# One transformer layer on one core: the LoRA rows transposed a tile later, next to the token transposes

## What is computed

```python
xA = jnp.einsum('bld,edr->bler', x, A)
xAB = jnp.einsum('bler,erd->bled', xA, Bm) * scale
return (xAB * w).sum(axis=2)
...
gate = x @ W_gate + _lora(x, sA_gate, sB_gate, scale) + _expert_lora(x, A_gate, B_gate, w, scale)
```

## Time and profile before

| what | value |
|---|---|
| median of 3 runs | 669.27 us (669.23 to 669.83) |
| profiled execution, its own time | 669.42 us |
| its span, first to last instruction | 667.6 us |
| TensorE busy | 659.3 us, 99% of the span |
| VectorE busy | 376.3 us, 56% |
| ScalarE busy | 257.8 us, 39% |
| GpSimd busy | 127.1 us, 19% |
| stage 1 on TensorE | about 8.9 to 128.9 us, tiles of 7.1 us (odd) and 8.0 us (even) |

### The profile page before, as it was taken

How to read it: one execution, slowest core, us unless ns; L and a number is a source line. 1 busy time by engine, 2 the same in 40 slices (tenths; PEclk the granted TensorE clock), 3 DMA queues, 4 the chain that set the end, 5 groups by cost and what they waited for, 6 DMA issues and landing times.

```text
span 667.6 us, 10326 instructions
## 1 busy us (share of the span) xinstructions
PE 659.3 (99%) x3568; PEld 545.4 (82%) x3568; DVE 376.3 (56%) x698; ACT 257.8 (39%) x413; POOL 127.1 (19%) x290
## 2 busy tenths in 40 slices
PE   7999999999999999999999999999999999999998
PEld 6899998877767788888888888888888888888886
DVE  6677888778676955434355443445344326534433
ACT  5434444566326323332343333243233324333321
POOL 3565676627336320000000000000000000000000
PEclk9999999999999999999999999999999999999999
DMA  6876665743745669930025000021400001300001
GB/s 215 311 256 212 214 235 194 261 183 149 292 170 196 236 183 3 77 128 0 1 79 221 32 0 0 0 75 72 184 0 0 0 8 71 127 0 0 0 0 63
DMA packets 41643, 74.21 MB, mean 111 GB/s; under 512 B 19393, under 2 KB 20289, under 8 KB 39953
## 3 DMA queue, kind: packets, MB, share of 16 engines
q1 hardware_dynamic: 38672, 64.52, 34.2%
q10 hardware_dynamic: 2736, 9.05, 3.4%
q0 software_dynamic: 208, 0.30, 0.3%
HBM read 52.81 MB, written 21.04 MB: 111 GB/s over the span
## 4 chain that ended last, share of the span: by engine, by line
PE 94%; DVE 3%; DMA 1%; ACT 1%; issue 0%; POOL 0%; DVEq 0%; POOLq 0%
PE bank L1246 21%; PE bank L1248 21%; PE bank L1247 21%; PE bank L1491 18%; PE bank L1464 6%; DVE den L1092 2%; PE bank L1477 1%; PE bank L1475 1%; PE bank L1265 1%; PE bank L1277 1%; DMA w_raw<-in_wkT 1%; PE bank L1364 1%; PE bank L1502 1%; PE bank L1504 1%; PE bank L1286 0%
## 5 line engine op out<-in xcount | busy, mean ns | idle before, releaser
L1246 PE MATMUL bank<-x,up_h 128*128 128x512 f32 (+1 forms) x352 | 137.1, 389 | 0.2 <-DVE x3r L1057 0.2
L1247 PE MATMUL bank<-x,up_h 128*128 128x512 f32 (+1 forms) x352 | 137.0, 389 | 0.0
L1248 PE MATMUL bank<-x,up_l 128*128 128x512 f32 (+1 forms) x352 | 137.0, 389 | 0.0
L1183 DVE TENSOR_TENSOR hf<-bank,silu 128x512 f32<-128x512 f32 x44 | 30.4, 691 | 155.0 <-issue 135.3
L1491 PE MATMUL bank<-dn,hid_h 128*128 128x512 f32 x352 | 108.8, 390 | 0.0
L677 ACT ACTIVATE hid_h<-hf 128x512 fp32r<-128x512 f32 x44 | 27.8, 632 | 144.1 <-DVE hf L1183 144.1
L1246 PEld LDWEIGHTS bank<-x,up_h 128*128 128x128 f32 x352 | 66.1, 188 | 14.4 <-issue 0.7
L1491 PEld LDWEIGHTS bank<-dn,hid_h 128*128 128x128 f32 x352 | 65.8, 188 | 14.5 <-DVE res L1208 0.6
L1248 PEld LDWEIGHTS bank<-x,up_l 128*128 128x128 f32 x352 | 66.1, 188 | 13.8
L1247 PEld LDWEIGHTS bank<-x,up_h 128*128 128x128 f32 x352 | 66.1, 188 | 13.7
L888 DVE TENSOR_TENSOR up_l<-up_raw,up_h 128x1024 fp32r<-128x1024 f32 x44 | 55.0, 1250 | 28.1 <-ACT up_h L677 28.1
(11 more groups left out here) (166 smaller groups left out, 1082.9 us busy)
## 6 DMA issues: line engine op xcount, KB each, us to landing
x<-scr_x SPq DMA_DIRECT2D x7, 2048.0 KB, 8.5
up_raw<-in_ffn_up SPq DMA_DIRECT2D x11, 768.0 KB, 7.4
scr_x<-xt ACTq DMA_DIRECT2D x16, 512.0 KB, 4.7
xin<-in_x SPq DMA_DIRECT2D x16, 256.0 KB, 4.9
scr_z<-zt SPq DMA_DIRECT2D x16, 256.0 KB, 2.1
x3r<-in_x SPq DMA_DIRECT2D x16, 256.0 KB, 3.1
scr_att<-x3r SPq DMA_DIRECT2D x16, 256.0 KB, 2.8
z<-scr_z SPq DMA_DIRECT2D x4, 1024.0 KB, 4.8
```

The costliest lines, as they stand in the source:

```text
L1183: nc.vector.tensor_tensor(hf[:], ps_u[:], silu[:], ALU.mult).then_inc(h_done, 1)
L1246: nc.tensor.matmul(dst, lh, rh, start=start, stop=False, **kw)
L1247: nc.tensor.matmul(dst, lh, rl, start=False, stop=False, **kw)
L1248: return nc.tensor.matmul(dst, ll, rh, start=False, stop=stop, **kw)
```

## The change

In tile t the LoRA rows of tile t-3, not t-2, are handled, and at other places: TensorE transposes them directly behind the token transposes, ScalarE rounds them behind the rounding of the values in mid-tile, VectorE takes the low halves behind `kf`, ahead of the normalising. Their weighting stays where it is. Tile 15 handles tile 12 in mid-tile and tile 13 at the end, as before. SyncE's stores come one tile later with it, and `tiles` now unrolls tiles 0 to 3 and loops over 4 to 7.

```diff
-            body(0, 0, 0)
-            body(1, 0, 1)
-            with eng.Fori(0, SPLIT_FROM // 2 - 1) as p:
-                body(2 * p + 2, p + 1, 0)
-                body(2 * p + 3, p + 1, 1)
+            for t in range(4):
+                body(t, t // 2, t % 2)
+            with eng.Fori(2, SPLIT_FROM // 2) as p:
+                body(2 * p, p, 0)
+                body(2 * p + 1, p, 1)
...
             with sp.Fori(1, GT) as p:
                 stage1(2 * p + 2, 0)
-                store_z(2 * p)
+                store_z(2 * p - 1)
                 x3a_load(p)
                 load_dn(2 * p)
                 stage1(2 * p + 3, 1)
-                store_z(2 * p + 1)
+                store_z(2 * p)
                 load_dn(2 * p + 1)
             for t in range(2 * GT + 2, TILES):
                 stage1(t, t % 2, more=(t + 3 < TILES))
                 if t < TILES - 1:
-                    store_z(t - 2)
+                    store_z(t - 3)
...
             x3_load(1)
             sp.wait_ge(kf_done, TILES)
             sp.dma_start(sa_dn[:], dram["sa_dn"]).then_inc(sa_in, 16)
-            for t in range(TILES - 3, TILES - 1):
+            for t in range(TILES - 4, TILES - 1):
                 store_z(t)
...
                 round_to(vf[:, s, 0:KD - 1, :, 0:DK], ps_va.rearrange("p (k h n) -> p k h n", h=HC, n=DK)).then_inc(va_done, 1)
+                if behind(t, 3):
+                    lora_out(t - 3)
                 if isinstance(t, int) and t in WQ_PART:
...
                 nc.scalar.activation(rexp[:], zraw[:, s, NZ - E:], ACT.Exp, scale=-1.0).then_inc(rexp_done, 1)
-                if behind(t, 2):
+                if isinstance(t, int) and t == TILES - 1:
                     lora_out(t - 2)
...
                 if isinstance(t, int) and t == TILES - 2:
                     heads_of(0)
+                if behind(t, 3):
+                    lora_lo(t - 3)
                 if ahead(t, 2):
                     normalise(t + 2, s)
...
-                if behind(t, 2):
+                if isinstance(t, int) and t == TILES - 1:
                     lora_lo(t - 2)
...
                 if ahead(t, 1) and not first:
                     transpose_tokens(t + 1)
+                if behind(t, 3):
+                    lora_transposed(t - 3)
                 if s == 0 and behind(t, 2):
...
-                if behind(t, 2):
+                if isinstance(t, int) and t == TILES - 1:
                     lora_transposed(t - 2)
```

More of the change, by code:

```diff
@@ L450, in _ @@
             sp.dma_start(w_raw[:, 0], dram["woT"]).then_inc(s2_in, 16)
-            store_z(0)
             x3a_load(0)
@@ L455, in _ @@
             sp.dma_start(w_raw[:, 1], dram["wqT"]).then_inc(s2_in, 16)
-            store_z(1)
+            store_z(0)
             load_dn(1)
```

## The result

The changed kernel took 674.5 us (median of 6, 674.0 to 675.8) where the kernel before took 669.4 (median of 6 in the same job): a ratio of 1.0078, 95% interval 1.0067 to 1.0089. That is 5.1 us more. The forecast was 671.9, range 670.3 to 673.5: the sign is right, the size is half of what came. In a second job the changed kernel took 673.8 us (4 executions, 672.5 to 675.2; ratio 1.0072, 1.0051 to 1.0093). The ten times scatter over 3.3 us; the six of the kernel before in the first job over 0.8.

What follows compares the result with a forecast made beforehand. TensorE was taken as the bound, busy 659.3 of 667.6 us. Two stalls at the end of tile 15 make it 2.5 us late, kvm adds 0.1: +2.6, saving included, so 671.9 us by the median; range 670.3 to 673.5.

Steps and rivals of the forecast that it cites:

- Part 1: TensorE, tiles 0 to 11: LoRA pairs merged behind the token transposes save 0.01 us each, 0.15 us taken in all.
- the 0.15 of the sum: TensorE at the end of tile 15: 0.15 us ahead through the merged transposes.
- rival C: Merged transposes on TensorE: saving 0.09 us a pair gives 670.9, entirely free pairs 669.3; chance 0.05.
- Part 2: VectorE and ScalarE in the steady tiles: VectorE's moved 0.95 us costs nothing, since TensorE waits for nobody there.
- Part 3: End of tile 15: TensorE stands 1.4 us until VectorE frees the shared PSUM bank; 1.26 us late net.
- Part 4: After tile 15: tile 12's store lands at 134.7 behind the 2 MB load; TensorE stands another 1.3 us at tile 14's transposes.
- the wait for kvm: Transposes of the keys-by-values product in the attention stage: TensorE waits another 0.1 us.
- the landing itself: Sync queue after tile 15: tile 12's store lands at 134.7, at latest 135.5, behind a load of 8.5 us.
- the 2.6 of the sum: Whole kernel: total added time of 2.6 us, with the 0.15 saved included.
- Rival A: Tile 12's store does not queue and lands at 132.1: no second stall, 670.5 us, or 669.6; chance 0.13.
- Rival B: TensorE's clock drops after the second stall and loses 1.6 us: 673.5, up to 673.8; chance 0.06.
- Everything later hangs on TensorE itself: Behind the attention stage's waits: TensorE has no idle time to swallow a shift, so the delay carries through.

Runs made afterwards that it cites:

- the two kernels that differ in it and have no second stall: Changed kernel with the 2 MB load behind the stores of tiles 12 and 13: 671.0 us; with tile 13's steps also moved into the attention stage: 669.95 us.
- the one with the eight instructions: Changed kernel with 8 semaphore-counting instructions added at the start of VectorE's program: 673.2 us, ratio 1.0062 to the kernel before.
- the run with more data ahead: Changed kernel with 1.15 MB of down weights loaded a second time directly behind the 2 MB load, ahead of tile 12's store: 680.3 us, ratio 1.0164.
- the kernel with neither stall: Changed kernel with the 2 MB load behind the stores of tiles 12 and 13, and tile 13's three steps moved into the attention stage: 669.95 us, ratio 1.0007.
- the unrolled one: Kernel before with only the loop altered: tiles 0 to 3 unrolled, loop over tiles 4 to 7; 669.5 us, ratio 1.0001.

## Why the prediction was right and wrong

**Part 1, the merge: right.** After, in tile 7, four token transposes, the pair and the next matmuls:

```profile
65.07 0.60 PE L1268 MATMUL bank<-ident_sb,xn 128*128 128x128 f32 x4
65.50 0.38 PE L1289 MATMUL bank<-ident_sb,zst 128*128 128x128 f32 x2
65.64 0.42 PE L1249 MATMUL bank<-va_h,xt 128*128 128x384 f32 x1
65.90 0.34 PE L1250 MATMUL bank<-va_l,xt 128*128 128x384 f32 x1
```

65.07 to 65.90 less the 0.17 of a 384-column matmul is 0.66 for six, 0.21 of it the pair, where the earlier trace rows gave 0.23 for a pair alone. From tile 0 to tile 14 TensorE gains 0.34 us (0.69 late, then 0.35); 0.23 of that is the pair that tile 2 no longer has (it comes back in tile 15), and 0.10 is the saving of 11 merges. It is no chance: from the one step to the other the nine traces of the changed order take 101.96 to 102.08 us, the four of the old order 102.25 to 102.38. At the end of tile 15 nothing is left of it: TensorE comes to the pair of tile 13 0.72 us late, where the start was 0.69, so the 0.15 of the sum was not there. The rival C, a larger saving, is out.

**Part 2: right.** TensorE has no wait in the tiles between tile 0 and tile 15.

**Part 3, the first stall: right in place and size.** 1.18 us measured, 1.4 forecast, and 1.1 us of time by the two kernels that differ in it and have no second stall. Where the second stands, it takes the first into itself.

**Part 4, the second stall: the mechanism right, one term mis-sized.** The chain from the landing to the pair of tile 14 is 140.04 - 136.46 = 3.6 us, as summed, and the wait for kvm behind it 0.2 instead of 0.1. The step that failed is the landing itself: I took one load of 8.5 us, and with it 134.7 for the landing of the store, and bounded it upward by 135.5, the one late store that the trace of before had. It was 136.4 in the first trace of the changed kernel and 134.3 and 134.6 in two others (the second and the one with the eight instructions). Of the 1.7 us too many in the first, 0.5 is that TensorE, and with it the issue, was late instead of ahead, which adds nothing to the stall, and 1.2 is the load, 9.7 instead of 8.5. Counted from the start of tile 0, the second kvm is 3.8, 2.2 and 2.7 us late in the three traces; the 2.6 of the sum, corrected by each trace's own load (9.7, 8.1, 8.5), gives 3.8, 2.2 and 2.6. So the chain is right to 0.1 us, and the size of its first term is not known beforehand. For the median this is not all: with the 8.5 us and the 0.6 us of the FFN it would be 672.5, and it was 674.5 and 673.8. What makes the 2 MB take 8.1 us in one execution and 9.7 in another, and half of it 7.6, stays open.

**Rival A** (the store does not queue) is out. **Rival B** (the clock) is probably in for a part. The changed kernel's executions with a mean granted clock of 0.997 took 675.8, 675.3, 674.8 and 675.2 us, the six with 0.999 or 1.0 took 672.5 to 674.5: 1.5 us apart in the mean, where the rival had 1.6. By an estimate 0.003 of 672 us is 4 us at half clock, worth up to 2. In the two traces of the changed kernel there is no such stretch (their executions had 1.0 and 0.999). That it follows the second stall in the four others is argued from the run with more data ahead and not seen in them, and one of 60 executions of the kernel before, which has no such stall, had 0.997 too (670.99 us).

**What was not in the sum at all:** 0.6 us in the FFN, which the prediction put at nothing ("Everything later hangs on TensorE itself, which has no idle time left that could swallow a shift"). With no wait recorded, VectorE's idle time before the first product of a group grows: 4.19 us instead of 3.81 in the second group, 3.95 instead of 3.81 in the third, 3.94 instead of 3.81 in the fourth (these three from the kernel with neither stall). That is 0.65 us, and what VectorE does behind it (the sums of the results) holds TensorE up by about the same, 0.4, 0.1 and 0.1 us. It comes with the changed program's instructions in their new places: the seven traces of kernels with the changed order and nothing put ahead of it have it, and no trace of the old order has it, the unrolled one included; it goes in both traces with eight instructions more ahead of the changed order and stays in the one with eight behind. That the place decides is shown; what in the place is not. The loading of instructions is the obvious candidate, and the traces point to it for the first and largest gap: in each of the seven a DMA of 8 KB of instructions (queue q14) starts 0.6 to 0.7 us after the start of the late product in the second group (in the kernel with neither stall at 349.1, the product at 348.47), and in none of the six others does one start within 3 us of that product. It is no proof, since the trace does not say for which engine the load is, and at the two small gaps there is none.

The tally of the first trace, 5.05 us at the last LoRA sum: 0.69 at the start (scatter); -0.34 to tile 14; +4.14 from there to the second kvm, which is 3.35 in the two stalls, 0.22 in the wait for kvm, 0.23 for the pair that comes back in tile 15, and 0.34 in steps too small to name; -0.06 to the FFN; +0.62 in it. The medians, 5.1 and 4.5 over before, need about as much without the start: the stalls and what hangs on them 2 to 4, the FFN 0.6, and the rest is not split further; slower loads and the lower clock of some executions are the likeliest parts of it.

## What to carry to other kernels

A step that is moved later in a loop has one iteration at the loop's end where two of its kind follow each other; follow their single buffers there, and ask for each wait on a DMA what has been issued ahead of it on the same queue. A small store behind a large load lands only after it, and since the time of such a load scatters by 2 us between executions, a sum that ends at such a landing needs a range from several landings and not from one. A stage that an edit does not touch can still move by a few tenths of a us, when the edit changes how many instructions lie ahead; pad the program before that is read as an effect of the idea.

## What the runs showed of the hardware

- The granted clock fell to 0.50 (1.2 GHz) in a stall of 6.3 us in the middle of the kernel and came back some 3 us after work was resumed, at a cost of 1.4 us; in the traces with stalls of 1.2, 2.2 and 2.3 us it stayed at 1.0.
- A 1 MB load took 7.6 us where 2 MB from the same tensor and on the same queue took 7.7 to 9.7 in the twelve traces that have the whole load.
- Eight instructions without work, ahead of everything on VectorE, take 0.38, 0.14 and 0.13 us of idle time off the first product of three groups of the FFN, 330 us and more later, and TensorE's shift in the FFN, 0.65 us, goes with it; the same eight at the end change nothing. In the kernel before they bring a gap of 0.4 us at 225 us.
